# A two-layer graph network on one core: small products, stored one-hot rows, and more columns copied on chip in the attention stage

## The reference, cut to what matters

```python
# layer 0, messages by an MLP
h = relu(concat([x[src], x[dst], edge_attr]) @ msg_W1 + msg_b1)
aggregated = segment_sum(h @ msg_W2 + msg_b2, dst)
x = x + layer_norm(h_in + MLP(concat([h_in, aggregated]))) * gamma + beta
# layer 1, attention with 4 heads of 32 channels, self loops added
z = leaky_relu(x_l[src] + x_r[dst], 0.2)
e = einsum('ehc,hc->eh', z, att)
alpha = softmax of e over the edges of one target
out = elu(segment_sum(alpha * x_l[src], dst) + bias)
```

## Time and profile before

| what | value |
|---|---|
| median of three runs | 3766.04 us |
| the profiled execution | 3759.81 us, its span 3758.0 us |
| busy share of the span: PE, DVE, ACT, POOL | 79%, 86%, 81%, 75% |
| mean granted TensorE clock | 0.889 |
| first and last gather of the message stage | 47.8 and 1862.1 us |
| first and last gather of the attention stage | 1881.5 and 3728.8 us |
| gathers, message and attention stage | 1436 and 1472 |

### The profile page before, as it was taken

How to read it: one execution, slowest core, us unless ns; L and a number is a source line. 1 busy time by engine, 2 the same in 40 slices (tenths; PEclk the granted TensorE clock), 3 DMA queues, 4 the chain that set the end, 5 groups by cost and what they waited for, 6 DMA issues and landing times.

```text
span 3758.0 us, 95339 instructions
## 1 busy us (share of the span) xinstructions
PE 2972.3 (79%) x19722; PEld 2526.9 (67%) x19852; DVE 3236.9 (86%) x21682; ACT 3038.1 (81%) x19868; POOL 2800.6 (75%) x2959
## 2 busy tenths in 40 slices
PE   6888888888888888888857777777777777777776
PEld 5777888788888878878745555555555555555554
DVE  5878778888788887888759999999999999999997
ACT  5878778888788787887658888888888888888884
POOL 6777777777777777777677777777777777777775
PEclk8878787887787787887789999999999999999999
DMA  7445455555455454555343333333333333333332
GB/s 197 141 141 147 138 143 142 151 144 142 144 146 146 142 146 142 144 145 145 92 130 89 90 90 90 90 91 90 91 91 90 91 91 90 91 90 91 90 91 57
DMA packets 368332, 440.78 MB, mean 117 GB/s; under 512 B 179205, under 2 KB 225635, under 8 KB 367743
## 3 DMA queue, kind: packets, MB, share of 16 engines
q1 hardware_dynamic: 274287, 243.84, 22.1%
q0 software_dynamic: 93056, 190.57, 19.5%
q10 hardware_dynamic: 400, 0.20, 0.0%
HBM read 411.03 MB, written 23.28 MB: 116 GB/s over the span
## 4 chain that ended last, share of the span: by engine, by line
POOL 40%; PE 17%; DVE 16%; issue 15%; ACT 7%; DVEq 2%; DMA 2%; ACTq 1%; SPq 1%; POOLq 0%
POOL t_ring L1067 37%; PE bank L1727 5%; DVE lone L1016 5%; PE bank L1703 4%; ACT lone L1769 4%; POOL m_ring L1055 3%; PE bank L1714 2%; DVE m_pre L1812 2%; DVEq L1003 1%; DVE m_hot_t L1795 1%; PE bank L1732 1%; DVE m_hot L1797 1%; ACT m_attr_t L1767 1%; DMA m_ring<-tab_a,src_t 1%; DVE acc L1827 1%
## 5 line engine op out<-in xcount | busy, mean ns | idle before, releaser
L1067 POOL DMA_INDIRECT t_ring<-tab_l,src_t x1472 | 1398.7, 950 | 468.0 <-issue 449.2
L1055 POOL DMA_INDIRECT m_ring<-tab_a,src_t x1436 | 1377.7, 959 | 449.2 <-issue 411.1
L1769 ACT ACTIVATE lone<-HT 128x4 uint8 x8704 | 864.9, 192 | 0.0
L2574 ACT ACTIVATE lone<-X 128x4 uint8 x7360 | 739.9, 189 | 70.3 <-issue 64.4
L1727 PE MATMUL bank<-w,m_attr_t 128*128 128x128 f32 x3128 | 705.6, 353 | 19.6 <-ACT m_attr_t L1767 13.1
L1727 PEld LDWEIGHTS bank<-w,m_attr_t 128*128 128x128 f32 x3128 | 607.8, 241 | 67.9 <-DVE m_hot L1797 22.6
L1016 DVE COPY lone<-HT 128x4 uint8 x7680 | 606.5, 192 | 0.0
L1703 PE MATMUL bank<-m_hot,m_hid 128*128 128x32 f32 x3128 | 485.1, 304 | 142.0 <-ACT m_hid L1758 102.9
L1703 PEld LDWEIGHTS bank<-m_hot,m_hid 128*128 128x128 f32 x3128 | 456.5, 224 | 191.8 <-ACT m_hid L1758 179.8
L2515 PE MATMUL bank<-t_hot_t,t_win 96*128 96x512 bf16 x391 | 148.0, 379 | 488.3 <-DMA t_ring<-tab_l,src_t 380.3
L2490 PE MATMUL bank<-t_a_edge,t_ring 128*128 128x128 f32 x3128 | 421.6, 279 | 2.9 <-DVE t_cd L2668 2.9
(11 more groups left out here) (268 smaller groups left out, 6063.9 us busy)
## 6 DMA issues: line engine op xcount, KB each, us to landing
m_ring<-in_edge_attr_dram SPq DMA_DIRECT2D x390, 256.0 KB
t_rows<-dst_rows SPq DMA_DIRECT2D x196, 256.0 KB
m_rows<-dst_rows SPq DMA_DIRECT2D x196, 192.0 KB
t_ring<-tab_l,src_t POOLq DMA_INDIRECT x1472
m_ring<-tab_a,src_t POOLq DMA_INDIRECT x1436
m_win<-tab_b SPq DMA_DIRECT2D x391, 24.0 KB
t_win<-tab_r SPq DMA_DIRECT2D x391, 24.0 KB
tab_b<-n_b SPq DMA_DIRECT2D x47, 96.0 KB
```

Of the source, the lines that this page charges most:

```text
L1055: pool.indirect_dma_start(out=r.got[u][0:rows, j, :], out_offset=None, in_=k.tab_a, in_offset=bass.IndirectOffsetOnAxis(ap=k.src_t[0:rows, ...
L1067: pool.indirect_dma_start(out=r.got[u][0:rows, j, :], out_offset=None, in_=k.tab_l, in_offset=bass.IndirectOffsetOnAxis(ap=k.src_t[0:rows, ...
L1769: pick_move(k, loaded.get(g), lambda out, col: act.activation(out, col, ACT.Copy), s["m_picked_s"])
L2574: late_move(k, loaded, lambda out, col: act.activation(out, col, ACT.Copy), s["t_pick_s"])
```

## The change

1. **Small products.** L1703 and L2490 are written as products with 32 stationary columns. In the message stage each j has four, one for each part of `hid`; in the attention stage each j has one for each head, with the head's own 32 columns of `a_edge`. So the diagonal blocks come out side by side in 32 columns, and DVE's four L2653 and its L2654 become one instruction on 128x64.
2. **Stored one-hot rows.** The message stage's comparison uses `win_id` (the window's rows as the attention stage has them, three copies), its ring has 4 buffers, not 2, and SP stores 32 of its rows for each group in DRAM (`hots`, 32 KB). In the attention stage SP loads them, broadcast over the four heads (128 KB for each group), into one of 8 buffers. DVE's comparison L2683 and the load of `dst_rows` there are gone.
3. **Picked groups.** In the attention stage the groups with g % 16 in 2, 5, 8, 11, 15 are picked, 18 <= g < 384: 115 groups. Their columns are copied in three slots (DVE 24, 20, 20 and ACT 20, 24, 20) or four (16 and 16 each).
4. **Addresses in two parts.** DVE loads 12 of a slot's addresses behind the logits, ahead of the sums, and the rest behind `zt`.

```diff
-VL = 4
-LATE_PICKED = P // VL
-LATE_BY_VECTOR = 12
+LATE_EVERY = 16
+LATE_IN = (2, 5, 8, 11, 15,)
+LATE_COLUMNS = {3: ((24, 20), (20, 24), (20, 20)), 4: ((16, 16), (16, 16), (16, 16), (16, 16))}
+LATE_SOONER = 4
+LATE_AHEAD = 12
...
-    return g % VL == VL - 1 and 2 * U <= g < k.groups // U * U
+    return g % LATE_EVERY in LATE_IN and 2 * U + 2 <= g < k.groups // U * U
...
+        def keep_marks(sp, g):
+            sp.dma_start(k.hots[g, :, :], hot_t[g % 4][0:W, :]).then_inc(s_put[g % 4], 16)
...   # message stage, SP, for each group g from 8 on; the last 8 behind the loop
                     load_targets(sp, g, u)
                     fetch_picked(sp, k, s, t["src"], g + 2)
+                    keep_marks(sp, g - U)
...   # message stage, TensorE
                     for j in range(J):
-                        pe.matmul(p_agg[q % 2][:, 0:W], lhsT=hid[q % 2][:, j, 0:P], rhs=hot[q % 4][:, j, :],
-                                  start=(j == 0), stop=(j == J - 1))
+                        for part in (slice(c * W, (c + 1) * W) for c in range(P // W)):
+                            pe.matmul(p_agg[q % 2][part, 0:W], lhsT=hid[q % 2][:, j, part], rhs=hot[q % 4][:, j, :],
+                                      start=(j == 0), stop=(j == J - 1))
...   # message stage, DVE
+                        if g >= 4:
+                            dve.wait_ge(s_put[g % 4], 16 * (g // 4))
-                        dve.tensor_scalar(hot_t[u % 2][0:3 * W, :], r.row[u], k.win3_id[0:3 * W, bass.ds(g, 1)],
+                        dve.tensor_scalar(hot_t[u % 4][0:3 * W, :], r.row[u], k.win_id[0:3 * W, bass.ds(g, 1)],
                                           None, ALU.is_equal)
...   # attention stage, SP
+            def load_marks(g):
+                after(sp, s["t_ep"], g + 1 - U)
+                sp.dma_start(r.hot[g % U][:], k.hots[g:g + 1, :, :].to_broadcast([H, W, EG])).then_inc(r.s_hot[g % U], 16)
...
                     load(sp, g, u)
+                    if rnd == 0:
+                        load_marks(g)
+                    elif g >= U + 2:
+                        load_marks(g - 2)
...   # attention stage, TensorE
                         for j in range(J):
-                            pe.matmul(p_nd[q % 2][:, 0:P], lhsT=r.got[g % r.deep][0:rows, j, :], rhs=a_edge[q % 2][0:rows, j, :],
-                                      start=(j == 0), stop=(j == J - 1))
+                            for h in range(H):
+                                own = slice(h * W, (h + 1) * W)
+                                pe.matmul(p_nd[q % 2][own, 0:W], lhsT=r.got[g % r.deep][0:rows, j, own],
+                                          rhs=a_edge[q % 2][0:rows, j, own], start=(j == 0), stop=(j == J - 1))
...
-                        hold(pe, s["t_masks"], g + 1)
+                        pe.wait_ge(r.s_in[q], 16 * (at[0] + 1))
+                        pe.wait_ge(r.s_hot[q], 16 * (at[0] + 1))
...   # attention stage, DVE
+                    if not tail:
+                        loaded = [late_load(nc, dve, k, s, rnd * U + u, 0, 0, LATE_AHEAD)]
...
-                        for h in range(H):
-                            own = slice(h * W, (h + 1) * W)
-                            dve.tensor_tensor(new[own, 0, :], p_nd[q % 2][own, own], shrink[q % 2][own, 1, :], ALU.mult)
-                        dve.tensor_tensor(new[:, 1, :], p_nd[q % 2][:, P:P + W], shrink[q % 2][:, 1, :],
+                        dve.tensor_tensor(new[:], p_nd[q % 2][:, 0:2 * W].rearrange("p (c w) -> p c w", c=2),
+                                          shrink[q % 2][:, 1, :].unsqueeze(1).to_broadcast([P, 2, W]),
                                           ALU.mult).then_inc(s["t_gap"], 1)
...
-                        dve.tensor_scalar(hot_t[q % 4][:], r.row[q], k.win_id[:, bass.ds(g, 1)], None,
-                                          ALU.is_equal).then_inc(s["t_masks"], 1)
```

More of the change, by code:

```diff
@@ L846, in edge_slots @@
     r.got = [r.ring[:, u] for u in range(deep)]
-    r.rows = [sb(f"rows{n}", [marks, 2, EG], I16) for n in range(U // 2)]
-    r.row = [r.rows[u // 2][:, u % 2, :] for u in range(U)]
+    if marks:
+        r.rows = [sb(f"rows{n}", [marks, 2, EG], I16) for n in range(U // 2)]
+        r.row = [r.rows[u // 2][:, u % 2, :] for u in range(U)]
+    else:
+        r.hot = [sb(f"hot{u}", [P, EG], BF16) for u in range(U)]
+        r.row = [r.hot[0][:].bitcast(I16)]
+        r.s_hot = [sems.one(f"{tag}_hot{u}") for u in range(U)]
     r.win = [sb(f"win{u}", [3 * W, P], BF16) for u in range(U)]
@@ L878, in late_picked, with late_picks, late_span, late_until @@
 def late_picked(k, g):
-    return g % VL == VL - 1 and 2 * U <= g < k.groups // U * U
[L883 to L890, removed]
+    return g % LATE_EVERY in LATE_IN and 2 * U + 2 <= g < k.groups // U * U
+def late_picks(k):
+    return [g for g in range(k.groups) if late_picked(k, g)]
+def late_span(k, g):
+    own = late_picks(k)
+    n = own.index(g)
+    return g - own[n - 1] if n else 3
+def late_until(k, g):
+    own = late_picks(k)
+    return g - (own[0] - late_span(k, own[0]))
@@ L900, in late_place, with late_load @@
-    after(act, s["t_pick_s"], (n - LATE_FIRST - 1) * VL)
+    n, g, i = now
+    act.wait_ge(s["t_ids"], 16 * (n + 1))
+    if n >= 2:
+        act.wait_ge(s["t_pick_v"], late_until(k, late_picks(k)[n - 2]))
+        act.wait_ge(s["t_pick_s"], late_until(k, late_picks(k)[n - 2]))
     act.activation(k.places[n % 2], k.ids[n % 2], ACT.Copy, scale=4.0, bias=float(k.x_at)
                    ).then_inc(s["t_places"], 1)
-def late_load(nc, eng, k, s, v, first, many):
-    n = late_number(k, v, 4)
-    if n is None:
-        return None
[L910 to L913, removed]
+def late_load(nc, eng, k, s, v, engine, start=0, stop=P):
+    now = late_being_picked(k, v)
+    if now is None:
+        return None
+    n, g, i = now
+    if i == 0 and start == 0:
+        eng.wait_ge(s["t_places"], n + 1)
+        after(eng, s["t_lone"], n - 1)
+    columns = LATE_COLUMNS[late_span(k, g)]
+    first = sum(a + b for a, b in columns[:i]) + engine * columns[i][0]
+    start, stop = first + start, first + min(stop, columns[i][engine])
@@ L924, in late_move @@
[L924 to L938, removed]
+    last = None
@@ new lines, in late_move, with late_fetch @@
+    for n, first, places in (some for some in loaded if some):
+        for q, place in enumerate(places):
+            last = move(k.lone[:, n % 2, first + q:first + q + 1].bitcast(U8),
+                        k.X[:].rearrange("p t d -> p (t d)").bitcast(U8)[:, bass.ds(place - k.x_at, 4)])
+    if last is not None:
+        last.then_inc(done, 1)
+def late_fetch(sp, k, s, src, v):
+    g = v + LATE_SOONER + 2
+    if not late_picked(k, g):
+        return
+    n = late_picks(k).index(g)
+    if n >= 2:
+        sp.wait_ge(s["t_places"], n - 1)
+    if n:
+        sp.wait_ge(s["t_ids"], 16 * n)
@@ L1154, in edges_mlp @@
         attr_t = [sb(f"m_attr_t{q}", [P, EG], F32) for q in range(2)]
-        hot_t = [sb(f"m_hot_t{q}", [P, EG], BF16) for q in range(2)]
+        hot_t = [sb(f"m_hot_t{q}", [P, EG], BF16) for q in range(4)]
+        s_put = [sems.one(f"m_put{q}") for q in range(4)]
         hot = [sb(f"m_hot{q}", [P, J, W], F32) for q in range(4)]
@@ L1664, in fast_sync @@
             rounds(sp, k.groups, body, 0)
+            for g in range(k.groups - U, k.groups):
+                sp.wait_ge(s["m_hp"], g + 1)
+                keep_marks(sp, g)
             nums = [one.num for one in k.early.all]
@@ L1671, in fast_sync @@
             sp_pair(sp)
+            for g in range(k.groups - 4, k.groups):
+                sp.wait_ge(s_put[g % 4], 16 * (g // 4 + 1))
             sp.wait_ge(s["n_bst"], 16 * (k.groups // U - 1))
@@ L2676, in body @@
                     if not tail:
[L2677 to L2684 removed]
+                        loaded.append(late_load(nc, dve, k, s, rnd * U + u, 0, LATE_AHEAD))
                     if not tail:
```

85 lines of the change are left out of this document (36 added, 49 removed).

## The result

The changed kernel takes 3727.65 us (median of four runs, 3726.28 to 3736.37) against 3764.35 us for the kernel before: ratio 0.991, 95% interval 0.9897 to 0.9922. The forecast was 3735 us. The profiled execution took 3726.28 us, its span is 3724.5 us, where the sum had 3728.4 us for the execution.

The account below looks back on a forecast made before the run. POOL's back-to-back gathers were taken to bound both stages; 28.9 us for gathers and 2.5 us for the tail came off: 3759.81 to 3728.4 us for the execution, 3766.04 to 3735 us for the median, range 3722 to 3800.

Parts of the forecast that it names:

- Picked groups: Attention stage: 115 instead of 92 groups skip their fourth gather, 23 gathers at 1.255 us, 28.9 us off POOL.
- DVE's need: Attention stage, DVE busy per group: 4.50 - 0.82 - 0.26 + 0.69 = 4.11 us of a 4.63 us period.
- Addresses in two parts: DVE's split address load in attention: 0.1 us exposed, between nothing and one whole load of 0.85 us a slot.
- Rival C: DVE's address loads show: 0.85 us exposed in each slot, DVE needs 4.96 us, about 3862 us; chance 0.03.
- Small products: PE, both stages: 32 pairs at 0.030 us take 0.96 us a group, bounds 0.028 and 0.111 us a pair; costs nothing.
- Rival A: TensorE becomes the bound: a small pair costs about 0.060 us, message stage 4.73 us a group, 3774 us; chance 0.15.
- A drain at a change of the tiling mode: PE in attention: lost overlap of 0.17 us twice a group, PE at 3.87 us, the sum unchanged.
- rival B: Small products lower PE's granted clock: 0.80 loses nothing, below 0.75 decides, 0.70 gives 3876 us; chance 0.04.
- Storing the rows: SP's stores and DVE's wait for them: 0, at most 6.7 us once; attention head 0 to 2 us, taken as 0.
- signs that the prediction named for being wrong: POOL waiting over 0.3 us for PE, `m_sum` or `m_hp`; no PE landed-row wait; attention clock under 0.75; DVE issue-idle before copies.
- The tail: Behind the last gather: about five groups' sums, some 0.6 us less each, 2.5 us in all, between 0 and 3.5.

Follow-up runs that it names:

- one_address_load: The changed kernel with all of DVE's addresses of a slot in one load behind `zt`: 3745.47 us, ratio 0.9965.

## Why the prediction was right, and where it was not

- **Picked groups** (28.9 us): right, in the mechanism and the size. The stage is 28.3 us shorter, and taking the picks back costs 28.2 us. In the 28.3 us are 4.1 us lost to the new wait (4.4 less the usual 0.3) and about 3.5 us won because gathers start every 1.253 us in the mean instead of every 1.256, as a gather took 0.948 us instead of 0.950.
- **DVE's need** (4.11 us a group): measured 4.12, and that the two agree is luck. The relief was taken as 1.08 us and is 0.90, the further copies as 0.69 us and are 0.52; the errors cancel. The sums took 0.25 us where 0.20 was taken, and a further copy costs less than the mean of the old ones. That the relief pays for the copies is right of the sums' instructions (without them 3877 us) and wrong of the comparison: without the stored rows DVE's 4.38 us still fit.
- **Addresses in two parts** (0.1 us): the second part shows nothing (1.7 us of issue ahead of the copies), the first at most 17.9 / 260 = 0.07 us, by the issue ahead of `t_old`. Of one load 0.48 us shows, between the bounds of 0 and 0.85. Rival C's mechanism is real, and it is the edit that keeps it away.
- **Small products** (0.96 us for 32 pairs, between 0.89 and 3.55): the value lies below the lower bound, 0.39 us. The bound counted one load of a quarter of the columns after another; in the one-block order a pair takes 26 ns, close to that bound, and in the order of the change 12 ns. Rival A is refuted: a load and a product together pass in 12 ns here. The Trainium skill (TensorE: Matmul & The Clock Gate, section "Wait — 56ns, not 53.3ns?") has about 62 ns for each MATMUL where microcode decodes it; no such limit is seen in this kernel. L2538 behind the small products takes 0.36 us instead of 0.17, also behind the slower order, and 0.17 us again with the large products back. A drain at a change of the tiling mode would look like this (the Trainium skill, TensorEngine Tiling (Array Packing), section Key Properties); that it is one is not shown. It was sized at 0.17 us for each side, and 0.19 us is what this side shows.
- **The clock** (rival B): it fell from 0.99 to 0.90 in attention, and PE's wait for landed rows still grew. No time was lost. In the message stage it rose, from 0.80 to 0.84.
- **Storing the rows** (0, at the head 0 to 2 us): DVE never waited for a store. The head cost more than its bound: one wait of 4.4 us, one of the signs that the prediction named for being wrong, though too small to move the forecast. The loads of `hots` stand between the stores of X on SP, and the last store is in the chain to ACT, PE and POOL. The wait is gone without the stored rows, and gone with the stores ahead.
- **The tail** (2.5 us, at most 3.5): 4.0 us. The sums on DVE gave more than the 0.6 us each that were worked out: 0.77 us, for five groups 3.8 us. PE's sums gave 0.31 us for each of the two groups that stand in both chains, and other links took some back.
- **The total**: 3728.4 us for the execution, measured 3726.3. The 2.1 us between them are 1.5 of the tail and 1.2 of a first gather that comes sooner, less 0.6 that the stage fell short. That the stage fell short by no more is luck, as shorter gathers nearly made good the new wait. The median was missed by 7 us, because the profiled execution of before lay 6.2 us under its median and that of after 1.4 us: the offset was carried over as if it were the kernel's.

What stays open: why the message stage's last gather starts anywhere between 1862.7 and 1869.6 us in kernels that don't differ there (its longest gather was 1.5 to 2.2 us); what makes the granted clock fall in one stage and rise in the other; and whether more picked groups in the message stage, where PE has 1.2 us to spare a group now, would carry the same 1.26 us for each gather. None of these was tried.

## What to carry to other kernels

When one engine issues without a gap from end to end, only its count matters: 23 gathers at 1.255 us gave 28 us of the span's 33.5, and other savings (0.6 us of PE and 0.26 us of DVE a group) gave nothing in the middle of a stage. Behind the last gather, where nothing is issued any more, the quicker sums did give time (4.0 us). A second engine at 95% busy is no bound as long as the first never waits for it, but it decides what may be moved onto it: add up its need per period with the address loads that nothing covers, and compare with the period that is aimed at. Idle time that another engine ends is slack, not need.

## What the runs showed of the hardware

- A float32 product with 128 rows, 32 stationary and 32 moving columns, with its weight load, follows the one before in 12 ns in the mean when the products go from one block of 32 partitions to the next (32 pairs in 0.39 us), and in 26 ns when four j stay in one block (0.83 us), both at the high clock. With 128 stationary columns it was 111 ns (8 pairs in 0.89 us).
- Two large products behind small ones took 0.36 us, and 0.17 us behind large ones.
- A load of 16 to 24 addresses on DVE's sequencer leaves 0.48 us a slot uncovered behind about 0.7 us of queued work (`one_address_load`); split at 12, at most 0.07 us. Loads of six took 0.81 and 1.42 us, longer than the 0.59 us of eight in the changed kernel.
- The granted clock of the attention stage was 0.99 before, 0.90 in the changed kernel, 0.94 with the same small products in the slower order and 0.96 with the large ones back. In the message stage it was 0.80 before, 0.84 in the changed kernel, 0.91 in the slower order and 0.80 with the large ones back. So small products went with a lower clock in one stage and with a higher one in the other.
